# Attention and feed-forward on one core: the maxima's DMAs and the loads of x issued by SyncE, in a new order

## The chip, the cores and the metric

One core of one Trainium2 chip runs the whole program. The metric is device time in microseconds; the kernel before took 1489.31 us, the median of 3 runs (1487.73 to 1489.78).

## What is computed

`x` has shape (16, 512, 256). Each layer normalizes its input and adds its result to `x`.

```python
def attention(x, w_att_val, wv_w, wv_b, out_w, out_b):      # x: layernorm(x); 16 heads of 16
    x_h = x.reshape(b, t, h, d).transpose(0, 2, 1, 3)
    xw = jnp.einsum('bhtd,hde->bhte', x_h, w_att_val)
    att = jnp.einsum('bhte,bhse->bhts', xw, x_h) / jnp.sqrt(d)
    att = jax.nn.softmax(att, axis=-1)
    vx = (x @ wv_w.T + wv_b).reshape(b, t, h, d).transpose(0, 2, 1, 3)
    o = jnp.einsum('bhts,bhsd->bhtd', att, vx)
    return o.transpose(0, 2, 1, 3).reshape(b, t, e) @ out_w.T + out_b

def ffn(x, w_gate, w_up, w_down):                            # 704 inner columns
    h = jax.nn.silu(fp4_linear(x, w_gate)) * fp4_linear(x, w_up)
    return fp4_linear(h, w_down)       # both operands rounded to FP4 in blocks of 16
```

## The kernel before

Three stages follow one another: a short first block (batch 0's inputs), attention over 16 batches (some 50 to 945 us), and the feed-forward layer over 64 tiles of 128 rows. The change is in attention alone.

**Work of a batch.** The 16 heads are taken in four quads of four heads, number i = 4b + g. A quad has four steps j, one for each 128 keys. In a step TensorE makes the scores of four heads, with keys on the partitions (L850), adds the negated maximum of each query with a second matmul from `max_stack` (L853, called the shift below), and ScalarE takes exponentials (L991). The weighing of values (L875) follows two steps at a time. In between TensorE computes the same scores with queries on the partitions, two quads ahead (`max_scores`, L842), from which VectorE takes the maxima (L1102), and the preparation of batch b + 1 and the finish of batch b - 1 (`IN_STEP`). These share four banks of PSUM (`ring`), so TensorE also waits for banks that VectorE frees.

**The way of the maxima.** The maxima of quad i + 1 are whole at the start of quad i. GpSimd splits them in a high and a low part (L626, L629), VectorE transposes them (`turn_maxima`, L1111), a DMA stores 16 KB to `max_rows` (`store_maxima`, waits for `m_turned`), and two DMAs of 8 KB load them into `max_stack` (`load_maxima`, waits for `max_stored`). There are two `max_turned` and two `max_stack`. `step_scores` waits for `max_loaded` ahead of step 0 of the quad.

**The way of x and q.** ScalarE copies the transposed half a of batch b + 1 out of PSUM (L1025, L1028), GpSimd splits it (L660, L662: `x_low`, `q_low`), SyncE stores it (four DMAs of 256 KB for x, two for q, L184), and once all six stores of a half have landed, loads stack g: two DMAs of 256 KB and four of 128 KB (`load_stacks`, L162, L172), which also waits until quad g of batch b has used its stack (`s_ready`). `max_scores` needs stack g of batch b + 1 two quads before the scores do.

**Who issues.** SyncE issues the stores of x and q, the stacks, and the weights' slabs. ScalarE issues `store_maxima` (after step 0), `load_maxima` (in the middle of step `LOAD_MAXIMA` = 2) and `load_x` (quad 1), between its exponentials:

```python
if k == QUAD // 2 and between is not None:
    between()
act.wait_ge(s_ready, QUAD * (TT * i + j) + k + 1)
```

SyncE's own order in a batch is that of its `batch(b)`: for g in 0 to 3, half g // 2 of batch b + 1 is stored at g = 0 and 2, then `s_ready` of quad g is waited for and stack g of b + 1 loaded; the weights' slabs follow at g = 3 and g = 1. Batches 1 to 12 run in a loop; batches 0 and 13 to 15 are written out. In batch 15 SyncE first loads the feed-forward weights.

Of the kernel before, what the change touches and what calls it, by code (L numbers as in the profile page):

```python
# [4 lines left out]
F32 = mybir.dt.float32  # L5
# [386 lines left out]
def attention_block(nc, ctx, x, max_rows, w_gate, w_up, w_down, slabs, slabs_kept, first_x,  # L392
# [15 lines left out]
    max_stack = [sb(f"max_stack{u}", [P, PAIRS, T], F32R) for u in range(2)]  # L408
# [9 lines left out]
    max_turned = [sb(f"max_turned{u}", [P, 2 * QUAD * TT]) for u in range(2)]  # L418
# [63 lines left out]
    def stands(kind, b):  # L482


        if not isinstance(b, int):
            return True
        if b < 0 or b > B:
            return False
        return {0: kind not in FINISH and kind != "weights", B - 1: kind not in PREPARE and kind != "weights",
                B: False}.get(b, True)  # L490

    def use(kind, b, kinds=ALL):


        order = [k for k in kinds if stands(k, b)]
        if isinstance(b, int):
            before = sum(stands(k, n) for n in range(b) for k in kinds)
        else:
            before = len(kinds) * b - sum(not stands(k, 0) for k in kinds)
        return before + order.index(kind)  # L500
# [48 lines left out]
    def prepared(c):  # L549

        return not isinstance(c, int) or c < B

    def quantizing(b):

        return not isinstance(b, int) or b < UNITS
# [22 lines left out]
    LOAD_MAXIMA = 2  # L578
# [3 lines left out]
    POOL_SET = ZEROED + 3 + ROWS + 2 * QUADS  # L582
    COPIES = 12

    def head_of(place):

        return 2 * (place % ROWS) + place // ROWS

    with nc.Block() as block:
# [146 lines left out]
        def _(sp):  # L736
            def store(c, a, dst, name, rows):

                sp.wait_ge(x_low if name[0] == "x" else q_low, HALVES * (c - 1) + a + 1)
                store_parts(sp, c, a, dst, rows, stored)  # L740

            def store_half(c, a):
                store(c, a, x_rows, f"x{a}", (xh, xl, xl, xh))
                store(c, a, q_rows, f"q{a}", (qh, ql))

            def batch(b):
                last = isinstance(b, int) and b == B - 1
                for g in range(QUADS):
                    i = QUADS * b + g
                    if not last:  # L750
                        if g % 2 == 0:
                            store_half(b + 1, g // 2)
                        sp.wait_ge(s_ready, QUAD * TT * (i + 1))
                        load_stacks(sp, b + 1, g, x_stack, q_stack, x_rows, q_rows, stored, stack_loaded)
                        if g == 3 and quantizing(b + 1):
                            sp.wait_ge(w_quantized, b + 1)
                            load_weights(b + 1)
                        if g == 1 and stands("weights", b):
                            store_weights(b)

            def load_weights(b):
                sp.dma_start(w_raw[:, :].rearrange("p (s c) -> p s c", c=P),
                             slabs[bass.ds(UNIT * b, UNIT)].rearrange("s p c -> p s c")).then_inc(w_loaded, 16)

            def store_weights(b):
                sp.wait_ge(kept_used, use("weights", b, BY_ACT) + 1)
                sp.dma_start(slabs_kept[bass.ds(UNIT * (b - 1), UNIT)].rearrange("s p c -> p s c"),
                             w_turned[:, :].rearrange("p (s c) -> p s c", c=P)).then_inc(w_stored, 16)

            def copy_weights():  # L770

# [39 lines left out]
                batch(b)  # L811
            batch(B - 3)
            batch(B - 2)

            sp.wait_ge(sum_used, use("v1", B - 2, BY_DVE) + 1)
            gate_up_T, down_T = ffn_weights(xn, splits)
            sp.wait_ge(w_stored, 16 * (1 + UNITS))
            sp.wait_ge(w_loaded, 16 * UNITS)
            gate_up_kept = slabs_kept[0:2 * I // P * HALVES].rearrange("(r a) p c -> a p r c", a=HALVES)
            for a in range(HALVES):  # L820
                sp.dma_start(gate_up_T[:, a, :].rearrange("p (r c) -> p r c", c=P), gate_up_kept[a])\
                  .then_inc(ffn_loaded, 16)
            down_kept = slabs_kept[2 * I // P * HALVES:SLABS].rearrange("(n k) p c -> k p n c", n=HALVES)
            for k, (_, width) in enumerate(FK):
                sp.dma_start(down_T[k][P - width:P, :].rearrange("p (n c) -> p n c", c=P), down_kept[k, 0:width])\
                  .then_inc(ffn_loaded, 16)
            batch(B - 1)
            sp.wait_ge(ffn_loaded, 16 * (HALVES + len(FK)))

# [153 lines left out]
        def _(act):  # L983
# [46 lines left out]
            def quad(b, g, first, last):  # L1030
                i = QUADS * b + g
                for j in range(TT):
                    loading = j == LOAD_MAXIMA and not (last and g == 3)
                    exponentials(i, j, first and g == 0,
                                 (lambda: load_maxima(i + 1, (g + 1) % QUADS)) if loading else None)
                    if j == 0 and not (first and g == 0):
                        end_half(i - 1, (g - 1) % QUADS)
                    if j == 2:
                        begin_half(i, g)
                    for kind in IN_STEP.get((g, j), ()):  # L1040
                        if stands(kind, b) and kind[:4] == "turn":
                            turn(kind, b)
                        if stands(kind, b) and kind[0] in "xq":
                            keep(kind, b + 1)
                        if stands(kind, b) and kind == "weights":
                            keep_weights(b)
                    if (g, j) == (2, 3) and quantizing(b):
                        weight_magnitude(b)
                    if (g, j) == (1, 0) and prepared(b + 3):
                        act.wait_ge(bn_done, TT * (b + 3))  # L1050
                        load_x(b + 3)
                    if j == 0 and not (last and g == 3):
                        store_maxima(i + 1, (g + 1) % QUADS)
                    if last and (g, j) in EARLY_ACT:
                        n = EARLY_ACT[g, j]
                        first_x.magnitude(act, n, n % 2)

            def store_maxima(i, g):

                act.wait_ge(m_turned, i + 1)  # L1060
                act.dma_start(max_rows[bass.ds(i, 1)].rearrange("o c r t -> (o r) c t"), max_turned[g % 2][:, :])\
                   .then_inc(max_stored, 16)

            def load_maxima(i, g):

                act.wait_ge(max_stored, 16 * (i + 1))
                if isinstance(i, int) and i < 2:
                    act.wait_ge(pool_set, ZEROED)
                rows = max_rows[bass.ds(i, 1)].rearrange("o (l h s) r t -> (o l) h (s r t)", l=2, h=QUAD)
                for m in range(ROWS):  # L1070
                    act.dma_start(max_stack[g % 2][KM * m:KM * m + 2, :, :].bitcast(F32),
                                  rows[:, PAIRS * m:PAIRS * m + PAIRS, :]).then_inc(max_loaded[g], 16)

            def load_x(c):
                act.dma_start(x_all[:, bass.ds(TT * c, TT), :],
                             x[bass.ds(c, 1)].rearrange("o (s p) e -> p (o s) e", p=P)).then_inc(x_loaded, 16)

            def batch(b):
                for g in range(QUADS):
                    quad(b, g, isinstance(b, int) and b == 0, isinstance(b, int) and b == B - 1)  # L1080

            load_q_stack(act, 0, 1, q_stack, q_rows, stack_loaded)
            store_maxima(0, 0)
            load_maxima(0, 0)
            load_x(2)
            batch(0)
            with act.Fori(1, B - 3) as b:
                batch(b)
# [562 lines left out]
```

## Time and profile before

| | |
|---|---|
| median of 3 runs | 1489.31 us |
| the profiled execution | 1486.98 us, its span 1485.1 us, mean granted clock 0.987 |
| busy in the span | TensorE 1422.1, its weight loads 882.9, VectorE 1267.9, ScalarE 866.0, GpSimd 659.4 us |
| DMA | SyncE's queue (q1) 137.08 MB, ScalarE's (q10) 10.51 MB |
| the chain that ended last | in the feed-forward layer: TensorE 33% of the span |

The profile names engines PE (TensorE's matmuls), PEld (its weight loads), DVE (VectorE), ACT (ScalarE), POOL (GpSimd), SP (SyncE); a q behind it is the engine's instruction queue, where DMAs are issued. A timeline row gives start, duration, line and tiles; in brackets stands how long the engine was idle before it and what ended that.

### The profile page before, as it was taken

How to read it: one execution, taken by the hardware profiler on the slowest of the kernel's cores; microseconds unless marked ns; L12 is line 12 of the kernel's file. 1: busy time of each engine (PE TensorE's matmuls, PEld its weight loads, DVE VectorE, ACT ScalarE, POOL GpSimd, SP SyncE). 2: the span in 40 equal slices, each digit the busy share in tenths (PEclk: the TensorE clock that was granted, in tenths of full speed). 3: DMA queues.
4: the chain of work that ended last, by engine and by line, in shares of the span. 5: the costliest groups of instructions: out<-in, count | busy, mean ns of one | idle time of the engine just before them, and what ended most of it. 6: DMA issues, size and time to landing. Idle time of an engine off the chain costs nothing. (4 is left out here: it accounts for less than half of the span.)

```text
span 1485.1 us, 32215 instructions
## 1 busy us (share of the span) xinstructions
PE 1422.1 (96%) x8562; PEld 882.9 (59%) x8562; DVE 1267.9 (85%) x2644; ACT 866.0 (58%) x1730; POOL 659.4 (44%) x910
## 2 busy tenths in 40 slices
PE   4699999999999999999999998899999999999998
PEld 2345555555555555555555554577777777777776
DVE  5788888888888888888888887599999999999995
ACT  1477777777777777777777777533333333333332
POOL 2346446446446445445545523234343343434341
PEclk7799999999999999999999999999999999999999
DMA  7655455455456456356356353000000000000000
GB/s 209 192 157 161 133 155 162 124 160 167 122 157 173 119 154 178 111 159 182 106 163 169 103 150 90 1 15 15 18 14 18 14 18 14 18 14 18 14 18 22
DMA packets 99433, 148.09 MB, mean 100 GB/s; under 512 B 20928, under 2 KB 58176, under 8 KB 99392
## 3 DMA queue, kind: packets, MB, share of 16 engines
q1 hardware_dynamic: 82272, 137.08, 32.4%
q10 hardware_dynamic: 17120, 10.51, 2.8%
q8 instruction: 21, 0.34, 0.1%
q14 instruction: 20, 0.16, 0.0%
HBM read 85.02 MB, written 65.27 MB: 101 GB/s over the span
## 5 line engine op out<-in xcount | busy, mean ns | idle before, releaser
L1102 DVE TENSOR_REDUCE neg_max<-ring 128x1 f32<-128x512 f32 x1024 | 642.6, 682 | 107.0 <-PE ring L842 103.3
L991 ACT ACTIVATE probs<-scores 128x512 f32<-128x512 f32 x1024 | 531.2, 602 | 186.2 <-PE scores L853 175.8
L1552 PE MATMUL gu_bank<-splits,f_x_T 128*128 128x352 f32 x1024 | 313.7, 459 | 0.1
L842 PE MATMUL ring<-x_stack,q_stack 64*128 64x512 f32 x1024 | 233.9, 455 | 30.5 <-DVE neg_max L1102 18.8
L875 PE MATMUL ring<-probs,v_quad 128*32 128x512 f32 x2048 | 246.2, 598 | 4.2 <-DVE neg_max L1102 4.1
L1552 PEld LDWEIGHTS gu_bank<-splits,f_x_T 128*128 128x128 f32 x1024 | 189.6, 190 | 95.4 <-ACT f_x_T L1526 0.5
L850 PE MATMUL scores<-q_stack,x_stack 64*128 64x512 f32 x1024 | 206.4, 398 | 4.9 <-DMA max_stack<-max_rows 2.6
L842 PEld LDWEIGHTS ring<-x_stack,q_stack 64*128 64x128 f32 x1024 | 98.3, 188 | 185.7 <-DVE neg_max L1102 138.1
L853 PE MATMUL scores<-max_stack,max_ones 64*128 64x512 f32 x1024 | 203.0, 392 | 0.0
L1308 POOL TENSOR_TENSOR f_small<-f_small,eps 128x1 f32<-128x1 f32 x64 | 43.0, 672 | 295.8 <-DVE f_small L1275 295.8
L649 POOL TENSOR_TENSOR pv_rows<-pv_more,pv_rows 128x512 f32<-128x512 f32 x63 | 80.8, 1283 | 180.8 <-ACT pv_more L997 180.8
L1511 ACT ACTIVATE h_T<-h_bank 128x512 f32<-128x512 f32 (+1 forms) x128 | 55.8, 488 | 176.1 <-PE h_bank L1562 176.1
L1570 PE MATMUL y_bank<-splits,h_T 128*128 128x256 f32 x640 | 148.9, 380 | 1.1 <-ACT h_T L1511 1.1
L875 PEld LDWEIGHTS ring<-probs,v_quad 128*32 128x32 f32 x2048 | 53.8, 109 | 125.5 <-issue 76.7
L1570 PEld LDWEIGHTS y_bank<-splits,h_T 128*128 128x128 f32 x640 | 116.7, 190 | 15.0 <-issue 0.8
L850 PEld LDWEIGHTS scores<-q_stack,x_stack 64*128 64x128 f32 x1024 | 97.5, 186 | 26.1 <-ACT probs L991 11.7
L853 PEld LDWEIGHTS scores<-max_stack,max_ones 64*128 64x128 f32 x1024 | 97.3, 186 | 21.0
L1359 POOL TENSOR_TENSOR hq<-h_level,h_scale 128x704 f32<-128x704 f32 x64 | 88.7, 1387 | 30.0 <-DVE h_level L1352 30.0
L626 POOL TENSOR_TENSOR max_cols<-neg_max,one 128x16 fp32r<-128x16 f32 x64 | 13.9, 218 | 190.2 <-DVE neg_max L1102 190.2
L1526 ACT ACTIVATE f_x_T<-x_bank 128x256 f32<-128x256 f32 x64 | 24.6, 384 | 117.6 <-PE x_bank L1540 117.6
L1346 DVE SCALAR_TENSOR_TENSOR h_level<-h_mag,h_units 128x704 f32<-128x704 f32 x64 | 57.1, 892 | 40.6 <-ACT h_mag L1341 40.6
L1518 ACT ACTIVATE gate<-gu_bank 128x352 f32<-128x352 f32 x128 | 58.8, 460 | 38.9 <-PE gu_bank L1552 38.8
(129 smaller groups left out, 1981.5 us busy)
## 6 DMA issues: line engine op xcount, KB each, us to landing
x_rows<-splits SPq DMA_DIRECT2D x128, 256.0 KB, 3.3
x_stack<-x_rows SPq DMA_DIRECT2D x128, 256.0 KB, 4.0
q_stack<-q_rows SPq DMA_DIRECT2D x248, 128.0 KB, 4.0
q_rows<-splits SPq DMA_DIRECT2D x64, 256.0 KB, 2.2
out_dram<-x_all SPq DMA_DIRECT2D x64, 128.0 KB, 1.7
x_all<-in_L_attn_x_dram ACTq DMA_DIRECT2D x14, 512.0 KB, 4.1
w_raw<-slabs SPq DMA_DIRECT2D x14, 192.0 KB, 3.9
slabs_kept<-w_turned SPq DMA_DIRECT2D x14, 192.0 KB, 3.8
```

Source lines behind the costliest of these rows:

```text
L649: pool.tensor_tensor(pv_rows[g % 2][:, :], pv_more[:, :], pv_rows[g % 2][:, :], ALU.add)\
L842: pe.matmul(bank(tiles[m])[:, :], row_tile(q_stack[q], m)[:, p, s * P:(s + 1) * P], row_tile(x_stack[q], m)[:, p, :], start=True, stop=Tru ...
L850: pe.matmul(scores[ROWS * p + m][:, :], row_tile(x_stack[g], m)[:, p, j * P:(j + 1) * P], row_tile(q_stack[g], m)[:, p, :], start=True, st ...
L853: pe.matmul(scores[ROWS * p + m][:, :], row_tile(max_ones, m)[:, 0, :], row_tile(max_stack[g % 2], m)[:, p, :], start=False, stop=True).th ...
L875: m = pe.matmul(bank(tile)[VW * h:VW * h + VW, :], v[q][:, j, h, :], probs[j][:, k, :], start=(j == steps[0]), stop=(j == steps[1]))
L991: act.activation(probs[j][:, k, :], scores[k][:, :], ACT.Exp).then_inc(p_ready, 1)
L1102: dve.tensor_reduce(neg_max[g % 2][:, at:at + 1], tile[:, :], AX.X, ALU.max, negate=True).then_inc(m_used, 1)
L1346: dve.scalar_tensor_tensor(out=level, in0=mag, scalar=SHIFT_MIN, in1=units, op0=ALU.max, op1=ALU.subtract)\
L1359: pool.tensor_tensor(blocks(out), blocks(level), spread(scale, BLK), ALU.mult).then_inc(done, 1)
L1518: act.activation(gate[1 - u][:, k, :], gu_bank[k][:, :], ACT.Silu).then_inc(gate_done, 1)
L1552: m = pe.matmul(gu_bank[c][:, :], x_T[u][:, a, :], gate_up_T[:, a, c * CH:(c + 1) * CH], start=(a == 0), stop=(a == HALVES - 1))
L1570: m = pe.matmul(y_bank[:, :], h_T[u][:, k, :], down_T[k][:, :], start=(k == 0), stop=(k == len(SLICES) - 1))
```

## The change

From batch 1 on SyncE issues what ScalarE issued: `store_maxima` and `load_maxima` for quads 1, 2 and 3 of the batch and quad 0 of the next, and `load_x(b + 3)`. ScalarE keeps those of batch 0 (and so the maxima of quads 0 to 4). The three functions get the issuing queue as an argument and are otherwise unchanged. SyncE's `batch(b)` is no longer a loop over g but a list: stack 3 of batch b now opens batch b, the four stores of half 1 of x go ahead of stack 1, and a store and a load of the maxima stand at four places each. The feed-forward weights are loaded in batch 15 behind the maxima of quad 1.

```diff
+            def store_x(c, a):
                 store(c, a, x_rows, f"x{a}", (xh, xl, xl, xh))
+
+            def store_q(c, a):
                 store(c, a, q_rows, f"q{a}", (qh, ql))
 
             def batch(b):
-                last = isinstance(b, int) and b == B - 1
-                for g in range(QUADS):
-                    i = QUADS * b + g
-                    if not last:
-                        if g % 2 == 0:
-                            store_half(b + 1, g // 2)
-                        sp.wait_ge(s_ready, QUAD * TT * (i + 1))
-                        load_stacks(sp, b + 1, g, x_stack, q_stack, x_rows, q_rows, stored, stack_loaded)
-                        if g == 3 and quantizing(b + 1):
-                            sp.wait_ge(w_quantized, b + 1)
-                            load_weights(b + 1)
-                        if g == 1 and stands("weights", b):
-                            store_weights(b)
+                first, last = isinstance(b, int) and b == 0, isinstance(b, int) and b == B - 1
+                i = QUADS * b
+                if not first:
+                    sp.wait_ge(s_ready, QUAD * TT * i)
+                    load_stacks(sp, b, 3, x_stack, q_stack, x_rows, q_rows, stored, stack_loaded)
+                    if quantizing(b):
+                        sp.wait_ge(w_quantized, b)
+                        load_weights(b)
+                    store_maxima(sp, i + 1, 1)
+                if not last:
+                    store_x(b + 1, 0)
+                if not first:
+                    load_maxima(sp, i + 1, 1)
+                if last:
+                    load_ffn_weights()
+                if not last:
+                    store_q(b + 1, 0)
+                if not first:
+                    store_maxima(sp, i + 2, 2)
+                sp.wait_ge(s_ready, QUAD * TT * (i + 1))
+                if not last:
+                    load_stacks(sp, b + 1, 0, x_stack, q_stack, x_rows, q_rows, stored, stack_loaded)
+                    store_x(b + 1, 1)
+                if not first:
+                    load_maxima(sp, i + 2, 2)
+                    if prepared(b + 3):
+                        sp.wait_ge(bn_done, TT * (b + 3))
+                        load_x(sp, b + 3)
+                if stands("weights", b):
+                    store_weights(b)
+                sp.wait_ge(s_ready, QUAD * TT * (i + 2))
+                if not last:
+                    load_stacks(sp, b + 1, 1, x_stack, q_stack, x_rows, q_rows, stored, stack_loaded)
+                if not first:
+                    store_maxima(sp, i + 3, 3)
+                    load_maxima(sp, i + 3, 3)
+                if not last:
+                    store_q(b + 1, 1)
+                    if not first:
+                        store_maxima(sp, i + 4, 0)
+                    sp.wait_ge(s_ready, QUAD * TT * (i + 3))
+                    load_stacks(sp, b + 1, 2, x_stack, q_stack, x_rows, q_rows, stored, stack_loaded)
+                    if not first:
+                        load_maxima(sp, i + 4, 0)
...
             def quad(b, g, first, last):
                 i = QUADS * b + g
                 for j in range(TT):
-                    loading = j == LOAD_MAXIMA and not (last and g == 3)
                     exponentials(i, j, first and g == 0,
-                                 (lambda: load_maxima(i + 1, (g + 1) % QUADS)) if loading else None)
+                                 (lambda: load_maxima(act, i + 1, (g + 1) % QUADS)) if first and j == LOAD_MAXIMA else None)
...
-                    if (g, j) == (1, 0) and prepared(b + 3):
+                    if first and (g, j) == (1, 0):
                         act.wait_ge(bn_done, TT * (b + 3))
-                        load_x(b + 3)
-                    if j == 0 and not (last and g == 3):
-                        store_maxima(i + 1, (g + 1) % QUADS)
+                        load_x(act, b + 3)
+                    if first and j == 0:
+                        store_maxima(act, i + 1, (g + 1) % QUADS)
```

How the order of instructions moves, in a batch whose code is written out (13), which has the order of the loop without its register work. On SyncE, before, from the stores of x half 0 to those of x half 1:

```order
L184 DMA x_rows<-splits 128x512 [waits x_low]
L184 DMA x_rows<-splits 128x512 x3
L184 DMA q_rows<-splits 128x512 [waits q_low]
L184 DMA q_rows<-splits 128x512
L162 DMA x_stack<-x_rows 64x1024 [waits stored0,s_ready]
L162 DMA x_stack<-x_rows 64x1024
L172 DMA q_stack<-q_rows 32x1024 x4
L162 DMA x_stack<-x_rows 64x1024 [waits stored0,s_ready]
L162 DMA x_stack<-x_rows 64x1024
L172 DMA q_stack<-q_rows 32x1024 x4
L767 DMA slabs_kept<-w_turned 128x3x128 [waits kept_used]
L184 DMA x_rows<-splits 128x512 [waits x_low]
```

The same stretch in the changed kernel, first to the stores of q half 0:

```order
L588 DMA max_rows<-max_turned 4x32x32 [waits m_turned]
L184 DMA x_rows<-splits 128x512 [waits x_low]
L184 DMA x_rows<-splits 128x512 x3
L598 DMA max_stack<-max_rows 2x1024 [waits max_stored]
L598 DMA max_stack<-max_rows 2x1024
L184 DMA q_rows<-splits 128x512 [waits q_low]
L184 DMA q_rows<-splits 128x512
```

and on to the stores of x half 1 and what follows them:

```order
L588 DMA max_rows<-max_turned 4x32x32 [waits m_turned]
L162 DMA x_stack<-x_rows 64x1024 [waits stored0,s_ready]
L162 DMA x_stack<-x_rows 64x1024
L172 DMA q_stack<-q_rows 32x1024 x4
L184 DMA x_rows<-splits 128x512 [waits x_low]
L184 DMA x_rows<-splits 128x512 x3
L598 DMA max_stack<-max_rows 2x1024 [waits max_stored]
L598 DMA max_stack<-max_rows 2x1024
L822 DMA slabs_kept<-w_turned 128x3x128 [waits kept_used]
```

A store of the maxima stands ahead of the stores of x half 0 and a load behind them; the stores of x half 1 have moved from behind stack 1 and the slab to directly behind stack 0, with the load for quad 2 behind them.

On ScalarE, before, quad 1 from the end of its step 0 on:

```order
L997 ACTIVATE pv_more<-ring 128x512 [waits pv_summed,pv_done]
L1061 DMA max_rows<-max_turned 4x32x32 [waits m_turned]
L991 ACTIVATE probs<-scores 128x512 [waits s_ready] x4
L1012 ACTIVATE w_turned<-ring 128x384 [waits w_stored,misc_ready]
L991 ACTIVATE probs<-scores 128x512 [waits pv_done,s_ready]
L991 ACTIVATE probs<-scores 128x512 [waits s_ready]
L1071 DMA max_stack<-max_rows 2x1024 [waits max_stored]
L1071 DMA max_stack<-max_rows 2x1024
L991 ACTIVATE probs<-scores 128x512 [waits s_ready] x2
L1002 ACTIVATE pv_rows<-ring 128x512 [waits pv_done]
```

and in the changed kernel:

```order
L1053 ACTIVATE pv_more<-ring 128x512 [waits pv_summed,pv_done]
L1047 ACTIVATE probs<-scores 128x512 [waits s_ready] x4
L1068 ACTIVATE w_turned<-ring 128x384 [waits w_stored,misc_ready]
L1047 ACTIVATE probs<-scores 128x512 [waits pv_done,s_ready]
L1047 ACTIVATE probs<-scores 128x512 [waits s_ready] x3
L1058 ACTIVATE pv_rows<-ring 128x512 [waits pv_done]
```

The store between steps 0 and 1 and the two loads in the middle of step 2 are gone; the exponentials of step 2 now follow one another.

## Rows read from the trace of the kernel before

**Rows 1.** One batch: busy us (count) by engine, TensorE clock, DMA share, GB/s
```profile
330.00:386.00 56.00, 55.05 (x393) 30.41 (x391) 48.48 (x94) 41.67 (x81) 29.43 (x41) 1.00 0.53 150
```

**Rows 2.** TensorE in time: first shift matmuls of quad 0, batches 7 to 9
```profile
445.52 0.39 PE L853 MATMUL scores<-max_stack,max_ones 64*128 64x512 f32 x2
...
501.55 0.40 PE L853 MATMUL scores<-max_stack,max_ones 64*128 64x512 f32 x2
...
557.76 0.39 PE L853 MATMUL scores<-max_stack,max_ones 64*128 64x512 f32 x2
```

**Rows 3.** Waits, 386 to 442 us: who waited for whom: us, times, longest
```profile
PEld ring L842 <- DVE neg_max L1102: 7.9, 11, 0.8
...
PE ring L875 <- DVE neg_max L1102: 0.4, 1, 0.4
...
PEld scores L850 <- ACT probs L991: 0.2, 1, 0.2
```

**Rows 4.** ScalarE in time, batch 8: start, us, what [idle before <-releaser]
```profile
509.18 0.25 ACTq L1071 DMA_DIRECT2D max_stack<-max_rows  x1
...
519.48 0.56 ACTq L1061 DMA_DIRECT2D max_rows<-max_turned  x1
520.15 2.07 ACT L991 ACTIVATE probs<-scores 128x512 f32<-128x512 f32 x4 [0.98 <-PE scores L853]
...
523.87 0.66 ACTq L1071 DMA_DIRECT2D max_stack<-max_rows  x2
524.65 1.09 ACT L991 ACTIVATE probs<-scores 128x512 f32<-128x512 f32 x2 [1.05 <-DMA max_rows<-max_turned]
...
546.85 0.55 ACTq L1061 DMA_DIRECT2D max_rows<-max_turned  x1
```

**Rows 5.** ScalarE's waits of the whole run, and TensorE in batch 15
```profile
ACT probs L991 <- DMA max_rows<-max_turned: 7.2, 5, 1.9
...
904.36 0.50 PE L850 MATMUL scores<-q_stack,x_stack 64*128 64x512 f32 x2 [0.60 <-ACT probs L991]
...
906.13 0.66 PE L915 MATMUL ring<-ident,o_rows 128*128 128x128 f32 x4 [0.78 <-DVE neg_max L1102]
```

**Rows 6.** SyncE's DMA issues in time, batch 8
```profile
511.19 1.96 SPq L184 DMA_DIRECT2D x_rows<-splits  x4
...
520.38 1.19 SPq L162 DMA_DIRECT2D x_stack<-x_rows  x2
521.67 1.96 SPq L172 DMA_DIRECT2D q_stack<-q_rows  x4
...
530.88 2.39 SPq L184 DMA_DIRECT2D x_rows<-splits  x4
```

**Rows 7.** Half-microsecond stretches of batch 8, columns as in rows 1
```profile
510.00:510.50 0.50, 0.50 (x12) 0.20 (x8) 0.50 (x2) 0.50 (x3) 0.50 (x1) 1.00 0.17 33
510.50:511.00 0.50, 0.50 (x12) 0.05 (x4) 0.50 (x2) 0.50 (x2) 0.50 (x2) 1.00 0.00 0
512.00:512.50 0.50, 0.50 (x8) 0.42 (x6) 0.50 (x1) 0.24 (x2) 0.50 (x2) 1.00 0.86 324
514.50:515.00 0.50, 0.48 (x7) 0.24 (x5) 0.50 (x2) 0.50 (x2) 0.42 (x2) 1.00 0.64 242
```

**Rows 8.** DMA issues from 510.9, 530.7 and 543.1 us: KB each, us to landing
```profile
x_rows<-splits SPq DMA_DIRECT2D x4, 256.0 KB, 2.3
...
x_rows<-splits SPq DMA_DIRECT2D x4, 256.0 KB, 3.8
...
q_stack<-q_rows SPq DMA_DIRECT2D x4, 128.0 KB, 4.0
```

**Rows 9.** TensorE in time: first score matmuls of quads 1 and 2, batch 8
```profile
515.33 0.39 PE L850 MATMUL scores<-q_stack,x_stack 64*128 64x512 f32 x2
...
529.49 0.40 PE L850 MATMUL scores<-q_stack,x_stack 64*128 64x512 f32 x2
```

**Rows 10.** GpSimd in time: end of the split of x, half 1, batch 8
```profile
521.68 1.30 POOL L662 TENSOR_TENSOR splits<-raw_x,splits 128x512 fp32r<-128x512 f32 x1
```

More of the change, by code:

```diff
@@ L583, in attention_block, with store_maxima, load_maxima, load_x @@
     COPIES = 12
+    def store_maxima(queue, i, g):
+        queue.wait_ge(m_turned, i + 1)
+        queue.dma_start(max_rows[bass.ds(i, 1)].rearrange("o c r t -> (o r) c t"), max_turned[g % 2][:, :])\
+           .then_inc(max_stored, 16)
+    def load_maxima(queue, i, g):
+        queue.wait_ge(max_stored, 16 * (i + 1))
+        if isinstance(i, int) and i < 2:
+            queue.wait_ge(pool_set, ZEROED)
+        rows = max_rows[bass.ds(i, 1)].rearrange("o (l h s) r t -> (o l) h (s r t)", l=2, h=QUAD)
+        for m in range(ROWS):
+            queue.dma_start(max_stack[g % 2][KM * m:KM * m + 2, :, :].bitcast(F32),
+                          rows[:, PAIRS * m:PAIRS * m + PAIRS, :]).then_inc(max_loaded[g], 16)
+    def load_x(queue, c):
+        queue.dma_start(x_all[:, bass.ds(TT * c, TT), :],
+                     x[bass.ds(c, 1)].rearrange("o (s p) e -> p (o s) e", p=P)).then_inc(x_loaded, 16)
     def head_of(place):
@@ L740, in store @@
                 store_parts(sp, c, a, dst, rows, stored)
-            def store_half(c, a):
+            def store_x(c, a):
                 store(c, a, x_rows, f"x{a}", (xh, xl, xl, xh))
+            def store_q(c, a):
                 store(c, a, q_rows, f"q{a}", (qh, ql))
             def batch(b):
-                last = isinstance(b, int) and b == B - 1
-                for g in range(QUADS):
-                    i = QUADS * b + g
-                    if not last:
-                        if g % 2 == 0:
-                            store_half(b + 1, g // 2)
-                        sp.wait_ge(s_ready, QUAD * TT * (i + 1))
-                        load_stacks(sp, b + 1, g, x_stack, q_stack, x_rows, q_rows, stored, stack_loaded)
-                        if g == 3 and quantizing(b + 1):
-                            sp.wait_ge(w_quantized, b + 1)
-                            load_weights(b + 1)
-                        if g == 1 and stands("weights", b):
-                            store_weights(b)
+                first, last = isinstance(b, int) and b == 0, isinstance(b, int) and b == B - 1
[42 more added lines that the diff above has]
+                        load_maxima(sp, i + 4, 0)
@@ L768, in store_weights, with load_ffn_weights @@
                              w_turned[:, :].rearrange("p (s c) -> p s c", c=P)).then_inc(w_stored, 16)
+            def load_ffn_weights():
+                sp.wait_ge(sum_used, use("v1", B - 2, BY_DVE) + 1)
+                gate_up_T, down_T = ffn_weights(xn, splits)
+                sp.wait_ge(w_stored, 16 * (1 + UNITS))
+                sp.wait_ge(w_loaded, 16 * UNITS)
+                gate_up_kept = slabs_kept[0:2 * I // P * HALVES].rearrange("(r a) p c -> a p r c", a=HALVES)
+                for a in range(HALVES):
+                    sp.dma_start(gate_up_T[:, a, :].rearrange("p (r c) -> p r c", c=P), gate_up_kept[a])\
+                      .then_inc(ffn_loaded, 16)
+                down_kept = slabs_kept[2 * I // P * HALVES:SLABS].rearrange("(n k) p c -> k p n c", n=HALVES)
+                for k, (_, width) in enumerate(FK):
+                    sp.dma_start(down_T[k][P - width:P, :].rearrange("p (n c) -> p n c", c=P), down_kept[k, 0:width])\
+                      .then_inc(ffn_loaded, 16)
             def copy_weights():
@@ L813, in _ @@
             batch(B - 2)
[L815 to L826, printed above, removed]
             batch(B - 1)
@@ L1056, in quad @@
                         first_x.magnitude(act, n, n % 2)
[L1058 to L1076, printed above, removed]
             def batch(b):
@@ L1082, in _ @@
             load_q_stack(act, 0, 1, q_stack, q_rows, stack_loaded)
-            store_maxima(0, 0)
-            load_maxima(0, 0)
-            load_x(2)
+            store_maxima(act, 0, 0)
+            load_maxima(act, 0, 0)
+            load_x(act, 2)
             batch(0)
```

## The prediction, made before the changed kernel was run

> **What bounds the kernel now.** I read the cut by batch first, then the waits of one batch, then the streams of instructions that the change touches, ScalarE's, SyncE's and TensorE's, and last the transfers. In a batch of attention TensorE is busy 55.05 of 56 us at full granted clock (1.00, the 2.4 GHz level), VectorE 48.48, ScalarE 41.67 [rows 1]. So attention is bound by TensorE, and a batch lasts what its first pair of shift matmuls shows: 445.52 to 501.55 is 56.03 us, 501.55 to 557.76 is 56.21 [rows 2]. What TensorE does wait for is VectorE: the weight loads wait 7.9 us in a batch for banks that the maxima's reductions free (most of it hidden, since weight loads run beside matmuls), and 0.4 us shows at the matmuls themselves. For ScalarE its score matmuls wait 0.2 us in a batch [rows 3].
>
> ScalarE therefore has room: 41.67 of 56 us, and most of the rest is waiting for scores. The change relieves an engine that does not set the end. What matters is what it does to the transfers on which TensorE waits.
>
> **What it takes from ScalarE.** In a batch four stores of 0.55 us, eight loads of about 0.25 us, one load of x, and the waits for a store's landing [rows 4]. Read quad 1 (a quad is four heads): the store goes at 519.48, and the next exponential starts at 520.15, right behind the end of that issue, so it may have been held up by some tenths. In batch 8 it waits 1.05 us more at 524.65 for the store [rows 4]; that batch is 0.18 us longer than the one before it. The whole trace has 7.2 us of such waits in 5 places; the largest that costs is in batch 15, where TensorE then stops for 0.60 and 0.78 us [rows 5]. Sum of the gain: batches 8 and 12 together 0.36, batch 15 1.4, and for the 3.3 us of waits that are left (7.2 - 2 x 1.05 - 1.8), early in attention, between 0.17 (0.18 of 1.05) and 0.77 (1.38 of 1.79) of each, from 0.6 to 2.6; I take 1.2. That is **3 us**. The plain issue time on ScalarE I cost at nothing: what covers it is ScalarE's own wait for scores. Its upper bound is the 0.2 us of a batch [rows 3], 3 us over 14 batches.
>
> **What it puts on SyncE's queue.** SyncE waits in order, and I take the transfers of its queue to land in order as well: the four stores of x land 2.3 us after issue where nothing is ahead of them and 3.8 us where a stack is [rows 8]. Each load of the maxima now stands behind whatever is ahead of it. Take batch 8 with its times as they are and go through the new order.
>
> The load for quad 1 (the first loop's store_x ahead of it). The stores of x can't go before the split on GpSimd is done, 511.19, and their four issues last to 513.15 [rows 6]. The two loads follow at about 513.3 and 513.7, where ScalarE issued the first at 509.18. The stores' traffic runs from 512.0 until between 514.5 and 515.0 [rows 7], the last landing 2.3 us after its issue at 512.8, about 515.1. A load with nothing beside it has no traffic any more 1.3 us after the first issue (509.18, gone by 510.5 [rows 4, 7]). So the loads land near 515.5; TensorE wants them at 515.33 [rows 9] and needs some 0.2 us to restart (a weight load). It comes 0.4 us late.
>
> The load for quad 2. Stack 0's first issue is at 520.38 and its last of six at about 523.3 [rows 6]. Those packets land 4.0 us after issue where no load of x runs beside them [rows 8], the last at 527.3. Then come the four stores of half 1 of x: ready at 522.98 [rows 10], before issued from 530.88 [rows 6], now directly behind the stack, 523.8 to 525.8. Four such stores alone kept the DMA engines busy from 512.0 to about 514.8 [rows 7], 0.7 us each, so they land until 527.3 + 2.7 = 530.0. The maxima's loads are issued at about 526.0 and 526.4 and land behind them, 530.4. TensorE wants them at 529.49 [rows 9]; with the restart it goes on at 530.6, **1.1 us late**. That contains the 0.4 us of quad 1, since the chain of stack 0 starts from q's split in quad 0, ahead of that wait.
>
> What of this comes back: while TensorE stands, VectorE works off its backlog, and some of the waits for it behind quad 2 shrink. I give that 0.25 us. So 0.85 us are lost in a batch. Batches 1 to 14 have the stores and the loads: 14 x 0.85 = **12 us**.
>
> The other two loads are early enough. For quad 3 the store goes behind stack 1 and SyncE waits for its landing, until about 538; the loads then land near 540, and quad 3 starts near 543. The store for quad 0 goes as now (546.85 [rows 4]), stack 2 is issued behind it instead of before it and lands at about 547.5 + 3.2 + 4.0 = 554.7, the loads behind it at 555, wanted at 557.5 [rows 2]. The stores' own landing was 4.4 us at worst beside other traffic (519.48 to 523.87 [rows 4]), and nothing but the double buffer waits for them otherwise. The load of x is used a batch later. In batch 15 the feed-forward weights now go behind the loads for quad 1; they are used from 946 us on, 35 us later.
>
> The edge of this term: below, the loads land 1.3 us after their issue at 526.4, as the lone ones did, and nothing is late: 0 us. Above, they take the 4.4 us that the store took beside traffic, in quad 1 as well: 513.7 + 4.4 = 518.1, 2.8 us a batch, 39 us. The middle is nearest to what the queue shows, whose transfers landed one behind the other. The Trainium skill ("DMA: Bandwidth & Descriptors", section on queues, rings and completion order) says that each issuing queue has a ring of its own on each DMA engine and the engine takes turns between rings. That speaks against this change: on ScalarE's queue a small load overtakes a megabyte on SyncE's, on SyncE's own it can't. No row here shows the turns packet by packet.
>
> **Sum.** The profiled execution took 1486.98 us (span 1485.1 and 1.9 around it), and 1486.98 + 12 - 3 = 1496. The median of the runs is 2.3 us above that execution; I forecast **1498 us**, 0.6% slower.
>
> **Rivals.**
> A, no load is late. The mechanism: the two loads are 16 KB and go to a few of the DMA engines, so they pass the tail of the stores and land before 529.3 in quad 2 and before 515.3 in quad 1. That is the point from which it decides. For it: the traffic of a lone load is over so fast [rows 7]. Against: the stores of x that wait for the stack ahead of them [rows 8]. It gives 1489.3 - 3 = 1486, and 1483 if the 3 us of plain issue time are paid out too. The same skill page, in "Issuing engines are not separate DMA queues", has it that the choice of the issuing engine saves only the time to issue, since all transfers interleave. By that rule A is what happens. Chance 0.21.
> B, the loads are late by 0.2 to 0.4 us only and the gain pays for it: 1488 to 1491. For it: both sides of the comparison at 529.49 rest on sums with an error of half a microsecond. Chance 0.13.
> C, the queue is later than I think: SyncE's issue with register work before each transfer, or stores that wait for stack 0 longer, so that quad 1 alone costs up to 2.8 us. 14 x 1.5 to 14 x 2.8, less 3: 1507 to 1525. Chance 0.16, of which the half is under 1511.
> My forecast, 0.85 us a batch with 0.5 to 1.3 around it, 1493 to 1504: 0.50.
>
> **Numbers.** Faster by over 0.2% (3 us, about what a measurement of this kernel can tell from no change) is A: 0.21. Within 0.2% is B: 0.13. Slower is the forecast and C: 0.66. Leaving out the far half of C and the far end of A, the range is 1484 to 1511.
>
> **What would show it.** TensorE's score matmuls at the start of quads 1 and 2 wait for the load of the maxima, in every batch from 1 on, near 0.4 and 0.7 us, and batches last 56.9 us instead of 56.03. The stores of x half 1 land just ahead of the second load. ScalarE has no DMA issues from batch 1 on, its wait for the maxima's store is gone, and batch 15 has no stop of TensorE at 904 to 906. I am wrong if these waits are missing (A), if batches are under 56.1 us, or if TensorE waits for a stack or for the loads of quads 3 and 0 instead.

## The result, and the profile after

The changed kernel took 1496.03 us, the median of 4 runs (1494.84 to 1497.06), beside 1488.52 us for the kernel before in the same runs: ratio 1.0051, 95% interval [1.0036, 1.0066]. It is 0.5% slower. The profiled execution's span went from 1485.1 to 1492.9 us.

The page after the change, busy times and the two queues: the maxima and x have moved to SyncE's queue (q1), and ScalarE's (q10) keeps what batch 0 and the first block issue. TensorE's busy time grew by 4.0 us (1422.1 to 1426.1).

```profile
PE 1426.1 (96%) x8562; PEld 884.9 (59%) x8562; DVE 1268.6 (85%) x2644; ACT 865.9 (58%) x1730; POOL 658.5 (44%) x910
...
q1 hardware_dynamic: 96868, 145.31, 34.1%
q10 hardware_dynamic: 2524, 2.28, 0.6%
```

TensorE in time, batch 8 after the change (start, us, line, tiles, [idle before <-releaser]). These are the first shift matmuls (L909, before L853) of quads 0, 1, 2 and of the next batch, and ahead of two of them the score matmuls (L906, before L850). They answer to [rows 2, 9]. The two rows of L898 are matmuls for the maxima, the first behind step 0 of quad 1, the second just ahead of quad 2.

```profile
505.28 0.40 PE L909 MATMUL scores<-max_stack,max_ones 64*128 64x512 f32 x2
...
519.66 0.51 PE L906 MATMUL scores<-q_stack,x_stack 64*128 64x512 f32 x2 [0.45 <-DMA max_stack<-max_rows]
520.00 0.40 PE L909 MATMUL scores<-max_stack,max_ones 64*128 64x512 f32 x2
...
522.88 0.50 PE L898 MATMUL ring<-x_stack,q_stack 64*128 64x512 f32 x2
...
533.34 0.50 PE L898 MATMUL ring<-x_stack,q_stack 64*128 64x512 f32 x2
533.86 0.50 PE L906 MATMUL scores<-q_stack,x_stack 64*128 64x512 f32 x2
534.19 0.40 PE L909 MATMUL scores<-max_stack,max_ones 64*128 64x512 f32 x2
...
562.25 0.40 PE L909 MATMUL scores<-max_stack,max_ones 64*128 64x512 f32 x2
```

Here is most of the change in time. From quad 0 to quad 1 it is 520.00 - 505.28 = 14.72 us, before 515.56 - 501.55 = 14.01. In front of quad 1 TensorE is idle for 0.45 us, and what ended that is the load of `max_stack`. Quad 1 to 2 took 14.19 us; before it was 14.16 in this batch, with ScalarE's wait for the store in it. No row shows a stop in front of quad 2, but the score matmul there comes 0.52 us behind the matmul ahead of it (533.34 to 533.86), where it is 0.34 us in front of a step without a wait: the load holds it there too, by some 0.2 us. The batch is 56.97 us. Over batches 2 to 12 the interval from quad 0 to 1 is 14.72 us in the mean (14.01 before), from quad 1 to 2 14.16 (between 13.91 and 14.55; before 14.07, between 13.98 and 14.50), and the other two are as before, 13.63 and 14.42. So a batch has grown by 0.81 us. The quad 1 to 2 interval has two kinds of batches: in 1, 3, 4, 5, 10 and 12 it is 13.91 to 13.93 us, in 2, 6, 7, 8, 9 and 11 it is 14.19 to 14.56. The load for quad 2 is late in half of the batches, the one for quad 1 in each of 1 to 12.

The waits of the whole run, with a line that the trace of before had only once (2.6 us in 1 place, batch 0's first quad):

```profile
PE scores L906 <- DMA max_stack<-max_rows: 9.0, 17, 2.6
```

Apart from batch 0's 2.6 us that is 6.4 us in 16 places: in front of quad 1 in batches 1 to 12 (0.41 to 0.46 us each), in front of quad 2 in batches 2, 7, 9 and 11 (0.16 to 0.38).

SyncE's issues of that batch, which answer to [rows 6]:

```profile
508.67 0.67 SPq L588 DMA_DIRECT2D max_rows<-max_turned  x1
514.89 1.96 SPq L184 DMA_DIRECT2D x_rows<-splits  x4
517.06 0.90 SPq L598 DMA_DIRECT2D max_stack<-max_rows  x2
521.30 0.94 SPq L184 DMA_DIRECT2D q_rows<-splits  x2
522.70 0.64 SPq L588 DMA_DIRECT2D max_rows<-max_turned  x1
524.08 1.31 SPq L162 DMA_DIRECT2D x_stack<-x_rows  x2
525.48 1.97 SPq L172 DMA_DIRECT2D q_stack<-q_rows  x4
527.70 2.07 SPq L184 DMA_DIRECT2D x_rows<-splits  x4
529.95 0.98 SPq L598 DMA_DIRECT2D max_stack<-max_rows  x2
```

The row at 514.89 is the stores of x half 0, at their old distance from the batch's start. The loads for quad 1 can only follow at 517.06, that is 11.78 us after the batch's first shift matmul; before it was 7.63 (509.18 - 501.55 [rows 2, 4]). Second, the stores of x half 1 (527.70) now follow stack 0 at once, and the loads for quad 2 (529.95) stand behind both.

Transfers issued from 523.9 to 530.9 us (KB each, median us to landing), which answer to [rows 8]: the stores of x behind the stack took 3.9 us, 2.3 where nothing was ahead.

```profile
x_rows<-splits SPq DMA_DIRECT2D x4, 256.0 KB, 3.9
x_stack<-x_rows SPq DMA_DIRECT2D x2, 256.0 KB, 3.8
q_stack<-q_rows SPq DMA_DIRECT2D x4, 128.0 KB, 3.9
```

### The profile page after: what moved, and what is told of

It reads as the page before. It is cut to its first block and busy times, and to the rows that moved or that the text cites. A ratio compares the mean times of both kernels' runs of the same rounds, so it can differ in the third digit from the quotient of the medians.

```text
span 1492.9 us, 32189 instructions
## 1 busy us (share of the span) xinstructions
PE 1426.1 (96%) x8562; PEld 884.9 (59%) x8562; DVE 1268.6 (85%) x2644; ACT 865.9 (58%) x1730; POOL 658.5 (44%) x910
## 5 line engine op out<-in xcount | busy, mean ns | idle before, releaser
L898 PE MATMUL ring<-x_stack,q_stack 64*128 64x512 f32 x1024 | 233.3, 454 | 29.1 <-DVE neg_max L1137 18.4
L906 PE MATMUL scores<-q_stack,x_stack 64*128 64x512 f32 x1024 | 207.4, 400 | 10.1 <-DMA max_stack<-max_rows 9.0
L898 PEld LDWEIGHTS ring<-x_stack,q_stack 64*128 64x128 f32 x1024 | 98.1, 188 | 182.2 <-DVE neg_max L1137 137.4
L909 PE MATMUL scores<-max_stack,max_ones 64*128 64x512 f32 x1024 | 202.9, 391 | 0.0
L906 PEld LDWEIGHTS scores<-q_stack,x_stack 64*128 64x128 f32 x1024 | 97.6, 186 | 33.6 <-issue 15.7
L909 PEld LDWEIGHTS scores<-max_stack,max_ones 64*128 64x128 f32 x1024 | 97.5, 186 | 20.7
```

The source lines that it names most:

```text
L898: pe.matmul(bank(tiles[m])[:, :], row_tile(q_stack[q], m)[:, p, s * P:(s + 1) * P], row_tile(x_stack[q], m)[:, p, :], start=True, stop=Tru ...
L906: pe.matmul(scores[ROWS * p + m][:, :], row_tile(x_stack[g], m)[:, p, j * P:(j + 1) * P], row_tile(q_stack[g], m)[:, p, :], start=True, st ...
L909: pe.matmul(scores[ROWS * p + m][:, :], row_tile(max_ones, m)[:, 0, :], row_tile(max_stack[g % 2], m)[:, p, :], start=False, stop=True).th ...
```

## The experiments

Intervals in the table are between first shift matmuls, the mean of batches 2 to 12 in the profiled execution. A ratio is to the runs of the kernel before that were made beside those of that kernel: their medians are 1488.52 us for the changed kernel, 1487.69 for the next four, 1488.97 for the two after these and 1487.85 for the last two.

| kernel | median, us | ratio to before, 95% interval | quad 0 to 1 | quad 1 to 2 | batch |
|---|---|---|---|---|---|
| before | 1488.52 | | 14.01 | 14.07 | 56.12 |
| changed | 1496.03 | 1.0051 [1.0036, 1.0066] | 14.72 | 14.16 | 56.93 |
| load 1 first | 1493.72 | 1.0038 [1.0024, 1.0052] | 14.01 | 14.70 | 56.77 |
| load 2 first | 1491.84 | 1.0026 [1.0016, 1.0037] | 14.72 | 13.92 | 56.69 |
| both first | 1485.02 | 0.9982 [0.9972, 0.9992] | 14.01 | 13.91 | 55.96 |
| order alone | 1488.26 | 0.9998 [0.9987, 1.0009] | 14.02 | 14.13 | 56.18 |
| late on ScalarE | 1522.56 | 1.0220 [1.0198, 1.0241] | 14.58 | 15.86 | 58.98 |
| weights late | 1486.96 | 0.9989 [0.9979, 1.0000] | 14.01 | 14.18 | 56.22 |
| queue alone | 1485.48 | 0.9982 [0.9973, 0.9992] | 14.01 | 13.92 | 55.97 |
| behind q too | 1596.77 | 1.0728 [1.0712, 1.0745] | 20.00 | 16.09 | 64.14 |

**Load 1 first.** In SyncE's `batch`, from the changed kernel:

```diff
-                if not last:
-                    store_x(b + 1, 0)
                 if not first:
                     load_maxima(sp, i + 1, 1)
+                if not last:
+                    store_x(b + 1, 0)
```

> The changed kernel, with the loads of the maxima of quad 1 ahead of the stores of x half 0 on SyncE's queue. Theory (each load is late for what stands ahead of it, and the load for quad 2 is tied to quad 0): the interval from quad 0 to quad 1 falls from 14.7 us to 14.0 in batches 2 to 12, but the load for quad 2 lands at the same distance from the batch's start, some 28.4 us, so the interval from quad 1 to 2 grows from 13.9-14.5 to about 14.6. The batch keeps most of its length and the time is 1493 to 1496. Rival (the two delays are independent and add): the batch loses 0.7 us, 11 batches or more, and the time is near 1487.

The theory held, with 1493.72 us. TensorE in batch 8 of this kernel, first shift matmuls of quads 0, 1 and 2, and its waits for the load in the whole run:

```profile
506.76 0.39 PE L909 MATMUL scores<-max_stack,max_ones 64*128 64x512 f32 x2
...
520.77 0.40 PE L909 MATMUL scores<-max_stack,max_ones 64*128 64x512 f32 x2
...
535.06 0.40 PE L909 MATMUL scores<-max_stack,max_ones 64*128 64x512 f32 x2
...
PE scores L906 <- DMA max_stack<-max_rows: 8.8, 12, 2.3
```

Quad 0 to 1 is 14.01 us again, and quad 1 to 2 has grown to 14.29 here and 14.70 in the mean. Of the 0.71 us saved at quad 1, 0.54 came back at quad 2. The second load was mostly hidden behind the first delay: with it gone, the load for quad 2 is late in each of batches 1 to 12, not in half of them.

**Load 2 first.** The same for the other load: `load_maxima(sp, i + 2, 2)` directly behind `load_stacks` of stack 0, `store_x(b + 1, 1)` behind it.

> The changed kernel, with the loads of the maxima of quad 2 ahead of the stores of x half 1. Theory: quad 0 to 1 stays at 14.7, quad 1 to 2 has no wait for the load and is 13.9 to 14.0; batches near 56.7, time about 1493 to 1495. Rival (the stall of quad 1 is absorbed and only quad 2's counts): the time falls to 1489 or under.

The step of 14.72 stays and 13.92 follows it without a wait; the mean batch is 56.69 us, as expected. The time, 1491.84, is 1 us under what I had named as the theory's, and above the rival's.

**Both loads first.**

> The changed kernel with both loads ahead of the stores of x. Theory: no score matmul waits for a load of the maxima, batches are 56.0 us or a little less, and what is left is the gain of the change alone, 2 to 5 us: 1484 to 1487. Rival (the longer batch comes from SyncE's other changes, such as stack 2 issued later or the earlier stores of x half 1 colliding with the stack): batches stay near 56.7 and the time above 1492.

1485.02 us, as expected, 0.18% under the kernel before, and both losses are gone. SyncE in batch 8, the two loads and the stores of x behind them:

```profile
506.27 0.69 SPq L598 DMA_DIRECT2D max_stack<-max_rows  x2
510.41 1.98 SPq L184 DMA_DIRECT2D x_rows<-splits  x4
...
523.08 0.68 SPq L598 DMA_DIRECT2D max_stack<-max_rows  x2
524.02 1.99 SPq L184 DMA_DIRECT2D x_rows<-splits  x4
```

TensorE's wait for the loads over the whole run is down to batch 0's:

```profile
PE scores L908 <- DMA max_stack<-max_rows: 2.6, 1, 2.6
```

So the loss is these two positions in the queue and nothing else of SyncE's new order, and what remains is the gain. In the batch, the first edit alone brings 0.16 us, the second alone 0.24, both together 0.97 (56.93 to 55.96).

**The new order alone**, with the maxima and x issued by ScalarE as before:

> The new order of SyncE without the maxima and the load of x on its queue: ScalarE issues those as in the kernel before. Theory: x half 1's stores ahead of stack 1 cost nothing by themselves, and the kernel is within 3 us of the one before (1486 to 1491); waits of ScalarE for the maxima's store may shorten or lengthen by tenths. Rival (the new order itself makes the loss): 1493 or more.

No change, 0.9998, as expected. The stores of x half 1 directly behind stack 0 cost nothing while no load of the maxima is behind them.

**Late on ScalarE.** The kernel just told, with the loads in the middle of step 3:

```diff
-    LOAD_MAXIMA = 2
+    LOAD_MAXIMA = 3
```

> As the run with the new order alone (ScalarE issues the maxima and the loads of x), and ScalarE issues the loads of the maxima in the middle of step 3 and not of step 2, which is about when SyncE issues them in the changed kernel (12 us after the first shift matmul of the quad). It tells apart the time of issue from the queue. Theory (the queue's order matters: a load on SyncE's queue waits for the transfers ahead): in quad 1 the load lands 1.5 to 1.8 us after its issue and not 2, and the delay at quad 1 is 0.2 to 0.4 us, not 0.7; in quad 2 there is little or none; 1488 to 1493. Rival (all queues share the engines alike, so only the time of issue counts): the delays are those of the changed kernel, time 1494 to 1497.

Both theories missed, with 1522.56 us. ScalarE's issues for quads 1 and 2 in batch 8 (the batch starts at 527.87), and TensorE at the starts of these quads:

```profile
538.94 0.25 ACTq L598 DMA_DIRECT2D max_stack<-max_rows  x1
...
553.11 0.26 ACTq L598 DMA_DIRECT2D max_stack<-max_rows  x1
```

```profile
542.06 0.50 PE L889 MATMUL scores<-q_stack,x_stack 64*128 64x512 f32 x2 [0.21 <-DMA max_stack<-max_rows]
...
557.59 0.50 PE L889 MATMUL scores<-q_stack,x_stack 64*128 64x512 f32 x2 [1.27 <-DMA max_stack<-max_rows]
```

The first load for quad 1 is issued 11.1 us after the batch's start, 0.7 us earlier than by SyncE, and TensorE goes on at 14.2, against 14.4 in the changed kernel (519.66 - 505.28). So a queue of its own brought next to nothing: 3.1 us from the first issue to TensorE, where SyncE's queue took 2.6. For quad 2 it is 557.59 - 553.11 = 4.5 us, on SyncE's queue 533.86 - 529.95 = 3.9. The queues' traffic shows why. From 553.1 to 555.9 us, 2.8 us from the first issue on, the only traffic is SyncE's 1.03 MB (first row: queue, packets, MB, share of the engines); the loads' eight packets on ScalarE's queue (q10) come from 555.9 to 556.5 us (the other two rows):

```profile
q1 hardware_dynamic: 629, 1.03, 102.5%
...
q1 hardware_dynamic: 265, 0.20, 102.7%
q10 hardware_dynamic: 8, 0.02, 7.0%
```

For quad 1 it is the same with 1.8 us and 0.66 MB (538.9 to 540.68 us). A small load on ScalarE's queue did not pass the megabytes on SyncE's.

The loss is larger than the change's: over before it is 0.57 us a batch at quad 1, 1.79 at quad 2 and 0.57 in the interval from quad 2 to 3. The load for quad 2, issued 25.2 us after the batch's start (24.7 by SyncE), is the latest; why it takes so much longer there was not tried. Behind the longest of these stops the granted clock fell too. In batch 2, the stop and the 3 us behind it (columns as in rows 1):

```profile
203.48 0.50 PE L889 MATMUL scores<-q_stack,x_stack 64*128 64x512 f32 x2 [2.85 <-DMA max_stack<-max_rows]
...
203.40:206.40 3.00, 2.92 (x14) 1.44 (x18) 0.76 (x3) 2.04 (x4) 0.00 (x0) 0.59 0.43 100
```

In batches 1, 2, 3 and 9 the clock is 0.58 to 0.73 there and quad 2 to 3 takes 15.3 to 15.4 us; in the others of batches 2 to 12 it takes 13.7 to 13.9, where it was 13.62 before.

**The feed-forward weights late**, in the kernel before:

```diff
             sp.wait_ge(sum_used, use("v1", B - 2, BY_DVE) + 1)
+            sp.wait_ge(max_loaded[1], 16 * ROWS * B)
```

> The kernel before, with the feed-forward weights loaded behind the landing of the maxima of quad 1 in batch 15. Theory: ScalarE's wait of 1.8 us in batch 15 and the two stops of TensorE go, the quad there is 13.1 us in place of 14.0, and the time falls by 0.8 to 1.4 us, which is about the noise: 1487 to 1488.5. Rival (the weights then come late or hit the maxima of quads 2 and 3): no gain or a loss of 1 us or more.

1486.96 us, ratio 0.9989 [0.9979, 1.0000]: the size fits and batch 15's quad takes 13.13 us as expected, but the interval ends at no change.

**The queue alone.** From the kernel with both loads first, x half 1 stored behind stack 1 as in the kernel before:

```diff
-                if not last:
-                    store_x(b + 1, 1)
...
                     load_stacks(sp, b + 1, 1, x_stack, q_stack, x_rows, q_rows, stored, stack_loaded)
+                    store_x(b + 1, 1)
```

> The kernel with both loads ahead of the stores of x, and the stores of x half 1 back behind stack 1: SyncE issues the maxima and the load of x, and otherwise nearly in its old order. Theory (queue and order are both harmless as long as no load of the maxima stands behind the stores of x): batches 56.0 us, the time that of the kernel with both loads first, 1484 to 1487. Rival (the earlier stores of x half 1 bring part of that kernel's gain): 1487 or more.

1485.48 us, the same as with both loads first. With the new order alone at no change, the gain is that of the move off ScalarE's queue and of batch 15's order; the new place of the stores of x half 1 has no part in it.

**Behind q too**, a larger dose: in the changed kernel `load_maxima(sp, i + 1, 1)` goes behind `store_q(b + 1, 0)`.

> The changed kernel with the loads of the maxima of quad 1 behind the stores of q half 0 as well: a larger dose of the suspected delay. Those two stores are issued 16.0 us after the first shift matmul of the quad and the last of them lands at 18.75. Theory (a load on the queue lands 0.2 us behind the last store ahead of it, TensorE goes on 0.15 us later): TensorE waits until 19.1, the interval from quad 0 to 1 is 19.3 to 19.6 in place of 14.7, the one from quad 1 to 2 has no wait and is 13.9; a batch grows by 4.4 us, and over 14 batches the time is near 1496 + 62 = 1558. Rival (a few tens of KB pass the stores, or the wait is absorbed by work that VectorE has left): the interval stays under 18 us and the time under 1540.

The direction was right and the size was not: 1596.77 us, where 1558 was expected. TensorE from the start of quad 1 to that of quad 2 in batch 5:

```profile
377.55 0.50 PE L898 MATMUL ring<-x_stack,q_stack 64*128 64x512 f32 x2
383.42 0.80 PE L906 MATMUL scores<-q_stack,x_stack 64*128 64x512 f32 x2 [5.36 <-DMA max_stack<-max_rows]
384.00 0.64 PE L909 MATMUL scores<-max_stack,max_ones 64*128 64x512 f32 x2
384.43 0.64 PE L906 MATMUL scores<-q_stack,x_stack 64*128 64x512 f32 x2
...
385.85 3.14 PE L931 MATMUL ring<-probs,v_quad 128*32 128x512 f32 x16
388.92 0.50 PE L898 MATMUL ring<-x_stack,q_stack 64*128 64x512 f32 x2
389.26 0.39 PE L906 MATMUL scores<-q_stack,x_stack 64*128 64x512 f32 x2
389.49 0.39 PE L909 MATMUL scores<-max_stack,max_ones 64*128 64x512 f32 x2
...
399.39 0.50 PE L898 MATMUL ring<-x_stack,q_stack 64*128 64x512 f32 x2
...
399.97 0.40 PE L909 MATMUL scores<-max_stack,max_ones 64*128 64x512 f32 x2
```

The stop is 5.36 us and TensorE goes on 19.3 us after the batch's start (364.12), 0.2 us later than expected. What comes on top is the clock. The pairs of matmuls behind the stop are 0.43 us apart where they are 0.23 before and later, and the block of 16 takes 3.14 us where it takes 1.92. The granted clock shows it (columns as in rows 1):

```profile
364.00:377.00 13.00, 12.43 (x95) 6.42 (x92) 11.93 (x25) 9.94 (x20) 7.77 (x11) 1.00 0.52 141
377.00:384.00 7.00, 1.62 (x9) 0.99 (x9) 1.92 (x4) 1.48 (x4) 2.75 (x4) 0.82 0.27 99
384.00:391.00 7.00, 7.00 (x41) 2.96 (x37) 2.95 (x6) 3.75 (x8) 1.19 (x1) 0.69 0.18 42
391.00:400.00 9.00, 8.69 (x63) 5.41 (x64) 7.96 (x19) 6.61 (x14) 4.53 (x8) 1.00 0.89 262
```

It is 0.82 in the stretch that holds the stop, 0.69 in the one behind it, so for part of both the lower of the two levels (1.2 and not 2.4 GHz), and 1.00 again from 391 us. This makes the first interval 19.88 us (364.12 to 384.00), where 19.3 to 19.6 were expected, and it is also why quad 2 is late, 16.09 us in the mean for 13.92. From the first shift matmul of quad 1 to the matmul behind step 0 it is 4.92 us here (384.00 to 388.92), 2.88 in the changed kernel (520.00 to 522.88); from there to the same matmul ahead of quad 2 it is 10.47 and 10.46 us (388.92 to 399.39, 522.88 to 533.34). So TensorE waited for nothing more there than in the changed kernel, and the 2.0 us are the slower clock. Over batches 1 to 13 the first of these pieces is 3.96 to 5.42 us long, and what follows it up to the first shift matmul of quad 2 is 11.0 to 11.2 in every one.

That accounts for the whole. A batch is 7.21 us longer than in the changed kernel, 5.28 at quad 1 (nearly all of it the stop) and 1.93 at quad 2 (the clock, less the changed kernel's waits there); 14 batches make 101 us, and the medians differ by 100.7. The expectation had the stop right to 0.2 us and nothing for the clock.

## Why the prediction was right

**The time.** 1498 us were forecast with 0.6% slower, measured were 1496.03 and 0.5%. The chance for slower was 0.66. The likeliest case was 1493 to 1504 us. The direction and the cause are the forecast ones; that the size came so near is in part luck, since three terms of the loss were off and cancelled.

**What bounds the kernel.** Right. To take the DMA issues off ScalarE is worth little: the kernel with both loads first gains 0.18%.

**The load for quad 1.** Right in its mechanism, short in its size: forecast 0.4 us late, measured 0.71. The issue was where I put it (11.78 us after the batch's start, forecast 11.75). What was short is the landing and the restart: the score matmul starts at 14.38, not at the 14.15 that 515.5 and 0.2 give, and the first shift matmul comes 0.34 us behind it where it was 0.23 before. That is 0.3 us more. The 0.23 us of the landing could have been read: the last of the four stores, issued at 512.82, lands 2.5 us later already in the trace of the kernel before (and in the changed kernel), and the 2.3 in the sum is the median of the four.

**The load for quad 2.** Forecast: both delays together 1.1 us in each batch, since quad 2's chain hangs on quad 0. The kernel with both loads first has the gain and none of the delays, so against it they can be read alone: 0.71 us at quad 1 (14.72 against 14.01) and 0.25 at quad 2 (14.16 against 13.91), 0.96 in all. Quad 2's part was forecast as 0.7 us in every batch; it is 0.3 to 0.65 in half of them and nothing in the others. TensorE went on at 28.58 in batch 8, not at 29.05. The last store of x behind the stack was issued at 529.37 and landed 4.2 us later, some 28.2 us after the batch's start; the 530.0 of the sum is 28.45. TensorE goes on 0.3 to 0.4 us behind that landing, where 0.4 for the load and 0.2 for the restart had been added. That the second delay is largely hidden by the first was shown by the run with load 1 first, where 0.54 of 0.71 us came back.

**What comes back.** 0.25 us were given for VectorE's backlog. Not seen: the intervals behind quad 2 are 13.63 and 14.42 as before. So the loss of a batch was forecast as 0.4 + 0.7 - 0.25 = 0.85 us and is 0.97 (56.93 against 55.96), of terms that were 0.3 too small, 0.45 too large and 0.25 too large a credit. In time the loss is the step from a ratio of 0.9982 to one of 1.0051, some 10 us, for 12 forecast.

**The gain.** Forecast 3 us, measured 2.7 (1485.02 against 1487.69, interval 1 to 4). In the trace of the kernel with both loads first batches 2 to 12 take 1.8 us less than before, of which the waits for the store were 0.9 and the rest is the fall of quad 1 to 2 from 13.98 us, the usual value without such a wait, to 13.91, some 0.08 us in every batch. It goes with the DMA issues on ScalarE, whose plain issue time was costed at nothing; that it is the issue time was not tried apart. Batch 15's first quad fell from 13.99 us to 13.14 in the changed kernel, 0.85 and not 1.4: the second of TensorE's stops, which waits for VectorE, is still there.

**Account of the changed kernel.** Batches 2 to 12 +8.9 us, 13 and 14 +0.7, batches 0 and 1 -0.9, batch 15 -0.9: +7.8, which is the growth of the span.

**The page on DMA.** The Trainium skill ("DMA: Bandwidth & Descriptors", queues, rings and completion order) says that each DMA engine takes turns between the queues' rings, packet by packet, and I had drawn from it that on a queue of its own a small load overtakes what SyncE has queued. The run late on ScalarE shows no such thing: nothing of the loads moved for 1.8 and 2.8 us after their first issue, while SyncE's queue moved 0.66 and 1.03 MB; a load with nothing beside it has its first traffic within 1.3 us [rows 4, 7]. What holds it back is not shown. Its other rule ("Issuing engines are not separate DMA queues") says that choosing the issuing engine saves only the time to issue, and nothing here speaks against that: what counted was when a load was issued and how much was under way then. But rival A, that I hung on it, doesn't follow from it: at quad 1 the load was late in each of batches 1 to 12, and at quad 2 in half of them.

**Rivals.** A is refuted by the 6.4 us of waits in 16 places behind batch 0, B by the interval of the ratio, C by the batches, of which none is 1.5 us longer. TensorE waited for no stack beyond batch 0's, and the loads for quads 3 and 0 were in time, as calculated. Of the signs named ahead, the waits of near 0.4 us at quad 1 and batches of 56.9 us came; the waits of near 0.7 us at quad 2 in every batch did not.

## What to carry to other kernels

Before a DMA is moved to another queue, go through that queue in order and write down, for each transfer, when it can be issued, what must land ahead of it, and when it is wanted. Small transfers that the bound engine waits for go ahead of big stores that nobody waits for yet: with two such lines moved, the same change is 0.18% faster than the kernel before, as good as any version of this study. When two transfers are late one after the other, mending one of them shows less than its part (0.16 or 0.24 us a batch, both together 0.97); mend both before you judge.

## What the runs showed of the hardware

**A long stop costs more than itself.** Behind stops of 5.4 us TensorE ran some 5 us at half speed (pairs 0.43 us apart, not 0.23), which cost 2.0 us in the batch shown. The same was seen behind four of the stops of the run late on ScalarE, among them that of 2.85 us. Behind the stops of under 0.5 us of the changed kernel the granted clock stayed 1.00.

**A second queue is no way past.** Loads of 8 KB on ScalarE's queue beside SyncE's 1 MB (quad 1) and 2 MB (quad 2) were no earlier than where they stood behind them (3.1 and 4.5 us from the first issue to TensorE, against 2.6 and 3.9); their packets moved 1.8 and 2.8 us after the first issue. How the engines choose between the queues was not measured.

**Profiled spans differ by some 2 us in code that no edit touches.** Batch 0 took 60.7 us in the changed kernel and 62.6 in the one with both loads first. The granted clock of the first batch (stretch from 50 to 107 us, changed kernel, then both first) was 0.91 in the one and 0.87 in the other:

```profile
50.00:107.00 57.00, 49.96 (x340) 26.78 (x338) 48.70 (x93) 37.67 (x72) 28.05 (x40) 0.91 0.57 164
```

```profile
50.00:107.00 57.00, 50.63 (x334) 27.07 (x334) 46.83 (x89) 35.80 (x69) 27.98 (x40) 0.87 0.57 166
```

The other runs with this code of batch 0 fall into the same two groups: 60.7 us with a clock of 0.92 (order alone), 62.6 to 63.0 with 0.88 (load 1 first, load 2 first, behind q too). The kernel before and the one with the weights late share their own batch 0, with 61.2 us at 0.92 and 63.1 at 0.88. Why the clock differs there is open. That is why intervals of batches were compared here, and medians of several runs, never two spans.
